# A coupling layer rewritten with kept twisted tokens and two scalars a token

## The reference

```python
def _twist(x):
    o_r, o_i, p_r, p_i = jnp.split(x, 4, axis=-1)
    return jnp.concatenate([p_r, -p_i, -o_r, o_i], axis=-1)
gf = _global_net(x.mean(axis=1, keepdims=True), ...)     # one number per sequence
out = x
for _ in range(3):                                        # cycles
    tf = _coupling_net(out, ...)                          # 128 -> 128 -> 64 -> 32 -> 1, one number per token
    combined = 0.7 * gf + 0.3 * tf
    coupling = BASE_COUPLING + adaptive_range * (combined - 0.5) * 2.0
    out = out + coupling * _twist(out)
# then: x = layernorm(x + out)
```

## Time and profile before

| | us |
|---|---|
| median of 3 runs | 946.77 |
| lowest, highest | 946.06, 952.11 |
| the profiled execution | 951.61 |
| its span, first to last instruction | 949.9 |

### The profile page before, as it was taken

How to read it: one execution, slowest core, us unless ns; L and a number is a source line. 1 busy time by engine, 2 the same in 40 slices (tenths; PEclk the granted TensorE clock), 3 DMA queues, 4 the chain that set the end, 5 groups by cost and what they waited for, 6 DMA issues and landing times. The chain is left out here.

```text
span 949.9 us, 20034 instructions
## 1 busy us (share of the span) xinstructions
PE 790.2 (83%) x7317; PEld 446.4 (47%) x7317; DVE 578.0 (61%) x1715; ACT 472.2 (50%) x750; POOL 295.8 (31%) x438
## 2 busy tenths in 40 slices
PE   1587999999837999369999999999999999739970
PEld 0233444444425777224555555555555555524430
DVE  4468798999651111245676766666676666324687
ACT  0386777878812222025555554444554555306664
POOL 3012233333427000234444443334334332100152
PEclk9999899999967999669999999999999999878995
DMA  0274234334204454121444443333444332220002
GB/s 26 72 234 129 71 98 109 78 97 104 68 28 122 145 145 120 49 77 46 97 96 96 96 92 86 71 78 83 76 96 90 84 85 52 52 50 1 1 0 89
DMA packets 111707, 78.05 MB, mean 82 GB/s; under 512 B 12272, under 2 KB 103088, under 8 KB 111616
## 3 DMA queue, kind: packets, MB, share of 16 engines
q1 hardware_dynamic: 107984, 71.16, 30.1%
q0 software_dynamic: 3344, 5.56, 2.2%
q10 hardware_dynamic: 288, 0.13, 0.1%
HBM read 37.86 MB, written 13.63 MB: 54 GB/s over the span
## 5 line engine op out<-in xcount | busy, mean ns | idle before, releaser
L1382 DVE TENSOR_REDUCE l_neg_max<-l_by_query 128x6 bf16<-128x768 f32 x128 | 122.5, 957 | 128.5 <-PE l_by_query L1128 128.0
L1454 POOL TENSOR_SCALAR_AFFINE_SELECT l_probs<-l_probs 128x512 f32<-128x512 f32 x128 | 86.9, 679 | 189.6 <-ACT l_probs L1257 189.4
L494 ACT ACTIVATE l_probs<-l_ps_s,minus_bound 128x1024 f32<-128x1024 f32 x128 | 137.3, 1114 | 2.2 <-PE l_ps_s L368 2.2
L1257 ACT ACTIVATE l_probs<-l_by_key 128x768 f32<-128x768 f32 x128 | 103.8, 811 | 66.4 <-PE l_by_key L1158 61.5
L1173 PE MATMUL l_ps_c<-l_probs,l_values 128*64 128x256 f32 (+1 forms) x1024 | 112.8, 342 | 0.0
L383 PE MATMUL l_ps_o<-l_probs,l_vpad 128*32 128x256 f32 x1024 | 81.5, 401 | 0.2
L1197 PE MATMUL l_ps_v<-w_o,l_ctx 128*128 128x128 f32 x512 | 68.5, 290 | 15.3 <-DVE l_ctx L1400 15.3
L1173 PEld LDWEIGHTS l_ps_c<-l_probs,l_values 128*64 128x64 f32 x1024 | 62.7, 137 | 39.4 <-issue 19.7
L1104 PE MATMUL l_ps_v<-w_v,l_xT 128*128 128x512 f32 x128 | 73.0, 652 | 0.2 <-ACT l_values L1278 0.2
L1197 PEld LDWEIGHTS l_ps_v<-w_o,l_ctx 128*128 128x128 f32 x512 | 62.5, 199 | 21.1 <-DVE l_ctx L1400 15.7
L1278 ACT ACTIVATE l_values<-l_ps_v 128x512 f32<-128x512 f32 x64 | 38.2, 597 | 68.2 <-PE l_ps_v L1104 68.2
(11 more groups left out here) (231 smaller groups left out, 1470.3 us busy)
## 6 DMA issues: line engine op xcount, KB each, us to landing
l_rrep<-rden_d SPq DMA_DIRECT2D x32, 512.0 KB
q_ring<-l_parts SPq DMA_DIRECT2D x192, 64.0 KB
k_ring<-l_parts SPq DMA_DIRECT2D x192, 64.0 KB
w<-in_L_ffn_w_dram SPq DMA_DIRECT2D x32, 256.0 KB, 3.0
disp_d<-zeros SPq DMA_DIRECT2D x8, 320.0 KB, 3.5
l_xin<-in_L_attn_x_dram SPq DMA_DIRECT2D x16, 128.0 KB, 2.7
l_xr<-in_L_attn_x_dram SPq DMA_DIRECT2D x16, 128.0 KB, 2.3
x_d<-l_x SPq DMA_DIRECT2D x16, 128.0 KB, 2.1
```

The costliest lines, as they stand in the source:

```text
L494: act.activation(probs[c % RING][:, :], ps_s[c % 2][:, :], ACT.Exp, bias=k["minus_bound"][:, :], scale=SCALE).then_inc(probs_sb, 1)
L1257: act.activation(probs[c % P_RING][:, :, 0:N + P], by_key[:, :, 0:N + P], ACT.Exp, scale=SCALE).then_inc(p_sb, 1)
L1382: dve.tensor_reduce(neg_max[:, :, half, :, h].rearrange("p a u -> p u a"), by_query[:, :, 0:3 * P].rearrange("p u (a q) -> p u a q", a=3), ...
L1454: pool.affine_select(out=corners, in_=corners, compare_op=ALU.is_ge, fill=0.0, base=0, pattern=[[0, 4], [1, P]], channel_multiplier=-1).th ...
```

## The change

- GpSimd makes `twisted`, the twist of all of `x3`, once at the start (`twist`: for each of the 8 groups a copy and a `tensor_scalar` of 128x256).
- Cycle 0 (`move_first`): VectorE computes `cur = coupling * twisted + x3`, one instruction of 128x128 for a block, 16 to a half.
- Cycle 1 (`move_second`): three small operations give the two scalars of a token after two cycles; GpSimd scales `x3` by one of them (`scale_second`, a `tensor_tensor` of 128x512 with a broadcast operand for each group), then VectorE adds `twisted` times the other, 16 instructions of 128x128. Two more small operations prepare the last cycle. `aside` and its copy back are gone.
- `twisted_moments`: VectorE sums `twisted` over the channels (4 instructions of 128x512 and 3 small ones for a half) for its mean and variance. It stands on VectorE right behind `move_second` of each half. The moments of `x3` come from `l1_layer`, which now keeps its `mv3` and `rstd3` for all blocks.
- Cycle 2: no tokens are moved for their own sake. `last_factors` computes, for a half at once, the scalars after three cycles, the variance of the sum from them, its power -1/2 (GpSimd, `root`, 128x16), two factors and `shift`. Then the result is `x3 * factor + shift` and, on top, `twisted * factor`. The first part is GpSimd's for half 0 (16 `tensor_scalar` of 128x128); for half 1 ScalarE makes 3 of every 4 blocks and GpSimd the fourth. The second part is VectorE's (`last_move`). The additions into `y` and the statistics are gone.
- The loops over cycles on TensorE and ScalarE are written out as six runs.

The diff, cut to its core:

```diff
+        twisted = sb("twisted", [P, ALL, C], FP32)
+        cur = sb("cur", [P, ALL, C], FP32)
+        coupling = sb("coupling", [P, CYCLES, ALL], FP32)
+        product = sb("product", [P, HB], FP32)
...
+            act.wait_ge(last_step, HALVES * LAST)
+            for g in range(GROUPS):
+                for j in range(ACT_BLOCKS):
+                    t = HB + g * GB + j
+                    last = act.activation(result[:, t, :], x3[:, t, :], ACT.Identity,
+                                          bias=shift[:, t:t + 1], scale=factors[:, 0, t:t + 1])
+                last.then_inc(by_act, 1)
...
+            dve.tensor_tensor(mean_sq[:, :], k["rstd3"][:, :], k["rstd3"][:, :], ALU.mult).then_inc(setup, 1)
+            dve.wait_ge(setup, SETUP - 1)
+            dve.tensor_tensor(moments[:, 0, :], mean_sq[:, :], k["mv3"][:, :, 1], ALU.mult).then_inc(setup, 1)
             dve.wait_ge(setup, SETUP)
+            moment = Steps(dve, moment_step, GROUPS + 3)
...
+            def twisted_moments(s):
+
+                m = moment.batch(s)
+                for g in range(GROUPS):
+                    blocks = slice(s * HB + g * GB, s * HB + (g + 1) * GB)
+                    m.did(dve.tensor_reduce(mean_t[:, blocks], twisted[:, blocks, :], AX.X, ALU.add))
+                m.wait()
+                m.did(dve.tensor_scalar(mean_t[:, of_half(s)], mean_t[:, of_half(s)], 1.0 / C, None, ALU.mult))
+                m.wait()
+                m.did(dve.tensor_tensor(mean_sq[:, of_half(s)], mean_t[:, of_half(s)], mean_t[:, of_half(s)], ALU.mult))
+                m.wait()
+                m.did(dve.tensor_tensor(moments[:, 1, of_half(s)], moments[:, 0, of_half(s)], mean_sq[:, of_half(s)], ALU.subtract))
+                m.end()
...
-                                         ALU.mult, ALU.add).then_inc(coupled, 1)
-                dve.wait_ge(coupled, 2 * n + 1)
-                dve.tensor_scalar(minus_coupling[:, :], coupling[:, :], -1.0, None, ALU.mult).then_inc(coupled, 1)
-                dve.wait_ge(coupled, 2 * n + 2)
+                                         ALU.mult, ALU.add).then_inc(couple_step, 1)
+                dve.wait_ge(couple_step, n + 1)
...
+            def move_first(n):
+                for g in range(GROUPS):
+                    dve.wait_ge(twisted_set, n * GROUPS + g + 1)
+                    for j in range(GB):
+                        t = n * HB + g * GB + j
+                        last = dve.scalar_tensor_tensor(cur[:, t, :], twisted[:, t, :], coupling[:, 0, t:t + 1], x3[:, t, :],
+                                                        ALU.mult, ALU.add)
+                    last.then_inc(moved, 1)
+            def move_second(n):
+                s = n % HALVES
+                half = of_half(s)
+                done = s * 4
+                dve.tensor_tensor(product[:, :], coupling[:, 0, half], coupling[:, 1, half], ALU.mult).then_inc(alpha_set, 1)
+                dve.tensor_tensor(straight[:, 1, half], coupling[:, 0, half], coupling[:, 1, half], ALU.add)\
+                   .then_inc(alpha_set, 1)
+                dve.wait_ge(alpha_set, done + 2)
+                dve.tensor_scalar(turned[:, 1, half], product[:, :], -1.0, 1.0, ALU.mult, ALU.add).then_inc(alpha_set, 1)
+                for g in range(GROUPS):
+                    dve.wait_ge(scaled, s * GROUPS + g + 1)
+                    for j in range(GB):
+                        t = s * HB + g * GB + j
+                        last = dve.scalar_tensor_tensor(cur[:, t, :], twisted[:, t, :], straight[:, 1, t:t + 1], cur[:, t, :],
+                                                        ALU.mult, ALU.add)
+                    last.then_inc(moved, 1)
+                dve.tensor_scalar(turned[:, 0, half], straight[:, 1, half], -1.0, None, ALU.mult)
+                dve.tensor_scalar(straight[:, 0, half], product[:, :], -1.0, 2.0, ALU.mult, ALU.add).then_inc(alpha_set, 1)
+                dve.wait_ge(alpha_set, done + 4)
+            def last_factors(n):
+                s = n % HALVES
+                half = of_half(s)
+                f = Steps(dve, last_step, LAST).batch(s)
+                twice = lambda a: a.unsqueeze(1).broadcast_to([P, 2, HB])
+                f.did(dve.tensor_tensor(both[:, :, :], turned[:, :, half], twice(coupling[:, CYCLES - 1, half]), ALU.mult))
+                f.wait()
+                f.did(dve.tensor_tensor(both[:, :, :], both[:, :, :], straight[:, :, half], ALU.add))
+                f.wait()
+                f.did(dve.tensor_tensor(squares[:, :, :], both[:, :, :], both[:, :, :], ALU.mult))
+                f.wait()
+                f.did(dve.tensor_tensor(squares[:, :, :], squares[:, :, :], moments[:, :, half], ALU.mult))
+                f.wait()
+                f.did(dve.scalar_tensor_tensor(var[:, :], squares[:, 0, :], EPS_LN, squares[:, 1, :], ALU.add, ALU.add))
+                dve.wait_ge(root_set, s + 1)
+                f.did(dve.tensor_tensor(factors[:, 0, half], both[:, 0, :], rstd[:, :], ALU.mult))
+                f.did(dve.tensor_tensor(factors[:, 1, half], both[:, 1, :], rstd[:, :], ALU.mult))
+                f.wait()
+                f.did(dve.scalar_tensor_tensor(shift[:, half], factors[:, 1, half], -1.0, mean_t[:, half], ALU.mult, ALU.mult))
+                f.end()
+            def last_move(s, g):
+                if s == 0:
+                    dve.wait_ge(by_pool, g + 1)
+                else:
+                    dve.wait_ge(by_act, g + 1)
+                    dve.wait_ge(by_pool, GROUPS + g + 1)
                 for j in range(GB):
                     t = s * HB + g * GB + j
+                    last = dve.scalar_tensor_tensor(result[:, t, :], twisted[:, t, :], factors[:, 1, t:t + 1], result[:, t, :],
                                                     ALU.mult, ALU.add)
+                last.then_inc(normed[s * GROUPS + g], 1)
...
 
             for s in two:
                 for g in range(GROUPS):
                     sums(s, g)
                 if s == 1:
+                    couple(0)
+                    move_first(0)
                 global_part(s)
+            couple(1)
+            move_first(1)
+            for n in (2, 3):
+                couple(n)
+                move_second(n)
+                twisted_moments(n % HALVES)
+            for n in (4, 5):
+                couple(n)
+                last_factors(n)
                 for g in range(GROUPS):
+                    last_move(n % HALVES, g)
         @block.gpsimd
         def _(pool):
+            def twist(group):
+                blocks = slice(group * GB, (group + 1) * GB)
+                x, to = (t[:, blocks, :].rearrange("p b (q w) -> p b q w", w=Q) for t in (x3, twisted))
+                pool.tensor_copy(to[:, :, 0:4:3, :], x[:, :, 2:0:-1, :])
+                pool.tensor_scalar(to[:, :, 1:3, :], x[:, :, 3::-3, :], -1.0, None, ALU.mult).then_inc(twisted_set, 1)
+            def scale_second(s, g):
                 blocks = slice(s * HB + g * GB, s * HB + (g + 1) * GB)
+                pool.wait_ge(alpha_set, s * 4 + 3)
+                pool.tensor_tensor(cur[:, blocks, :], x3[:, blocks, :],
+                                   turned[:, 1, blocks].unsqueeze(2).broadcast_to([P, GB, C]), ALU.mult).then_inc(scaled, 1)
+            def root(s):
+                pool.wait_ge(last_step, s * LAST + 5)
+                pool.tensor_tensor(rstd[:, :], var[:, :], k["minus_half"][:, 0:1].broadcast_to([P, HB]), ALU.pow).then_inc(root_set, 1)
+            def scale_last(s, g, blocks):
+                pool.wait_ge(last_step, (s + 1) * LAST)
+                for j in blocks:
+                    t = s * HB + g * GB + j
+                    last = pool.tensor_scalar(result[:, t, :], x3[:, t, :], factors[:, 0, t:t + 1], shift[:, t:t + 1],
+                                              ALU.mult, ALU.add)
+                last.then_inc(by_pool, 1)
+            for group in range(HALVES * GROUPS):
+                twist(group)
+            for s in two:
                 for g in range(GROUPS):
+                    scale_second(s, g)
+            for s in two:
+                root(s)
+                for g in range(GROUPS):
+                    scale_last(s, g, range(GB) if s == 0 else range(ACT_BLOCKS, GB))
```

More of the change, by code:

```diff
@@ L1562, in _, with turn @@
         def _(pe):
-            def turn(n, s, src, g):
+            def turn(n, g):
+                src, s = (x3 if n < HALVES else cur), n % HALVES
                 at_least(pe, moved, (n - 2) * GROUPS + g + 1)
@@ L1630, in run @@
                 layer1(n, 3)
-            run(0, 0, x3, before=False)
-            pe.wait_ge(setup, SETUP)
-            global_net(0)
-            run(1, 1, x3)
-            global_net(1)
-            with pe.Fori(1, CYCLES) as cycle:
-                for s in two:
-                    run(cycle * 2 + s, s, cur)
-            layer2(2 * CYCLES - 1, 1)
-            layer3(2 * CYCLES - 1)
-            layer4(2 * CYCLES - 1)
+            for n in range(RUNS):
+                run(n)
```

(42 more changed lines are left out.)

179 lines of the change are left out of this document (60 added, 119 removed).

## The result

Median of 11 runs 941.95 us (938.97 to 947.02), and 946.77 (942.88 to 952.11) for the kernel before: ratio 0.994, interval 0.9921 to 0.9959, thus 3.9 to 7.5 us less of 947. The forecast was a median of 942.9, which is 3.85 less, and a change of under 1%.

What follows compares the result with a forecast made beforehand. VectorE was taken to set the end of the coupling layer, the last 97 us. Step by step the end moved from 946.74 to 942.9, 3.85 us less, carried over to the median of 946.77: 942.9 (-0.4%), range 937 to 949.6.

Steps and rivals of the forecast that it cites:

- step 3: Cycle 1, first half: GpSimd's scaling at 1.24 each holds VectorE's moves up; TensorE gets the second group 0.85 us late.
- step 1: Start: GpSimd's 16 twist instructions of some 0.4, 6.3 us, needed 15 us later at the first coupling, cost nothing.
- The lock: Cycle 1: VectorE gets one instruction through per GpSimd tensor_tensor, taken at 1.24 us; GpSimd isn't slowed.
- step 6: Half 0's end: coupling 0.26, dependent operations 1.25, power 2.9, GpSimd's 16 scalings 5.1, hold-ups 1.2; done at 931.9.
- Steps 3 to 5: Cycle 1 up to the last cycle's first coupling: held-up moves and moments make that coupling 4.4 us later.
- Step 7: Half 1's end: chain 4.9, ScalarE's 12 blocks 4.95, VectorE's last four 1.15; 11.0 us instead of 13.2 + 2.1.
- Rival A: Cycle 1: GpSimd's scaling doesn't hold VectorE up; the last cycle's first coupling 4.4 us earlier, thus 938.5; chance 0.22.
- Rival B: Half 0's end, slower: GpSimd's two-scalar tensor_scalar costs 0.74, 6.7 us more, 949.6; loses from 0.56 each; chance 0.18.

## Why the prediction was right

The forecast held in sign and mechanism. In size it was short: 3.85 us less were forecast, 5.4 measured (60.1 against 58.6 from the second tanh). That it is off by only 1.5 is in part luck: it was 2.6 too high up to coupling 4 and 1.1 too low behind it, and these errors cancel in part. The 0.9 us of the clock in the first 18 us of the layer wasn't forecast and is not in these numbers.

*The bound* was read rightly: half 1 follows half 0 in VectorE's order, and the tanh of the last run is long there. After the change it is still so (920.87 against 925.77), though in half 0 VectorE now waits for GpSimd's power and scalings.

*Prices.* The power: 2.9 forecast, 2.93 and 2.90 (the line through 0.73 and 1.03 gives 2.8 to 2.85, rounded up in the forecast). The wide moves: 0.265 forecast, 16 in 4.3. GpSimd's `tensor_tensor` in step 3: I took 1.24, the copied price of a full operand; with the broadcast it is 1.03. That is 0.8 us too much in each half, as the experiment with a full operand shows. GpSimd's `tensor_scalar`: 0.32 forecast, 0.43 apart measured, inside the bounds of 0.22 and 0.74. I took it from copy and select, and the trace had nothing nearer. The same kind of price was wrong in step 1: the 16 instructions of the twist took 9.4 us and not 6.3, since eight of them, L1861, take 0.85. They end at 858.1, 11 us before the first move that needs them, so it cost nothing.

*The lock*, VectorE's moves held up by GpSimd's instructions. Three held-up moves in each half, as the rows of before had it, each as long as one `tensor_tensor`. In step 6 my 0.1 for each of 12 is 0.13 for about six: 1.2 forecast, 0.8 measured (7.75 less 16 times 0.43). The moves are held up there as well: two of them last 0.53 and not 0.35.

*Steps 3 to 5* had the right consequences, smaller: the turns of run 5 wait 0.9 for VectorE and not 2 to 3, tanh 4 comes 0.85 late instead of 3.0, coupling 4 1.8 late instead of 4.4. 0.8 a half is the price above, 0.4 a half the small operations and sums (3.0 and 0.2 where I took 3.25 and 0.4).

*Step 6* was 12.5 forecast, 13.8 measured, from the 0.43. *Step 7* was 11.0, and 10.8 measured. Together that is 1.1 too low behind coupling 4.

*Rival A* (VectorE not held up) didn't happen, but making it happen with VectorE's own scaling gave only 0.7 us, not 4.4. A counted from a coupling 4 that was 4.4 late, and it was 1.8 late; most of that was the moments. And A had GpSimd scale beside VectorE for nothing, where here VectorE spends 0.2 for each block on it. GpSimd scaling beside an unhindered VectorE wasn't tried. *Rival B* didn't happen at two scalars. At one scalar GpSimd's scaling takes 0.60, past my 0.56 at which the change should lose; the length was 60.5 then, still 3.4 under the kernel before (63.9), since the other terms had come out cheaper.

The sentence of the Trainium skill in "GPSIMD Engine Reference", "Engine selection", that work with one input is roughly line rate on GpSimd fits the copy (0.40 for 256 columns) and not the multiplication: 0.375 to 0.60 for 128 columns, 0.85 for 256 (L1861 in the groups above). VectorE does the one-scalar one at one every 0.2, where GpSimd takes 0.60. And by "SBUF — State Buffer", "Who interferes with whom", the power, which reads SBUF, should have held VectorE's moves, which have two inputs there, up; eight moves went through in 2.18 us beside it.

## What to carry to other kernels

Price an operation with a broadcast operand, or with another number of stages, only from a row of that very form: on GpSimd these were 17% (1.06 against 1.28) and up to 60% (0.60 against 0.375) apart. Small work that stands in an engine's order ahead of a step on the path (the moments) costs what of it is left when that step's input is there, here 1.0 of 3.0 us each time, and nothing where the engine idles; look for that place first. To judge a change of half a percent at the end of a program, measure the changed stage from an event that repeats, and not the span.
